# ODE stage of a convolution-attention hybrid: matmuls that stream 28 columns, 24 of them zeros, in place of 4

## The reference, cut to what matters

```python
def _mlp(y, W1, b1, W2, b2, W3, b3):
    h = jnp.tanh(y @ W1.T + b1)
    h = jnp.tanh(h @ W2.T + b2)
    return h @ W3.T + b3

def _rk4_step(y, dt, params):
    f = lambda z: _mlp(z, *params)
    k1 = f(y)
    k2 = f(y + dt / 2 * k1)
    k3 = f(y + dt / 2 * k2)
    k4 = f(y + dt * k3)
    return y + dt * (k1 + 2 * k2 + 2 * k3 + k4) / 6
```

## Time and profile before

| what | value |
|---|---|
| runs of the kernel, median (lowest to highest) | 7657.05 us (7656.08 to 7659.73) |
| the profiled execution, its own time | 7654.61 us |
| the profiled execution, span from first to last instruction | 7652.8 us |
| mean granted PE clock | 0.567 |
| busy: PE, DVE, ACT, POOL | 6975.1, 4228.9, 3810.8, 1229.8 us |
| matmuls at L851 with H, L851 with L, and L830 | 130816, 8176, 57232 |

### The profile page before, as it was taken

How to read it: one execution, slowest core, us unless ns; L and a number is a source line. 1 busy time by engine, 2 the same in 40 slices (tenths; PEclk the granted TensorE clock), 3 DMA queues, 4 the chain that set the end, 5 groups by cost and what they waited for, 6 DMA issues and landing times. The chain is left out here.

```text
span 7652.8 us, 407459 instructions
## 1 busy us (share of the span) xinstructions
PE 6975.1 (91%) x201629; PEld 6431.8 (84%) x144393; DVE 4228.9 (55%) x21034; ACT 3810.8 (50%) x26434; POOL 1229.8 (16%) x5230
## 2 busy tenths in 40 slices
PE   8884999999999999999999999999999998638886
PEld 3221999999999999999999999999999997427774
DVE  5444555555555555555555555555555554448997
ACT  3331555445544554455445554455445543328886
POOL 1000222112211221222112221122112221010001
PEclk7785555555555555555555555555555555658897
DMA  1000000100010001000100001000100000012332
GB/s 49 1 20 30 4 4 4 43 5 4 4 43 5 4 4 43 5 4 4 43 5 4 4 4 43 5 4 4 43 5 4 4 23 5 0 53 111 121 123 81
DMA packets 45001, 186.93 MB, mean 24 GB/s; under 512 B 7155, under 2 KB 27318, under 8 KB 33030
## 3 DMA queue, kind: packets, MB, share of 16 engines
q1 hardware_dynamic: 38662, 145.18, 4.9%
q0 software_dynamic: 4480, 15.38, 0.6%
HBM read 122.93 MB, written 37.62 MB: 21 GB/s over the span
## 5 line engine op out<-in xcount | busy, mean ns | idle before, releaser
L851 PE MATMUL p<-H,W 128*128 128x4 f16 x130816 | 5594.8, 168 | 36.7 <-ACT h L938 20.3
L851 PEld LDWEIGHTS p<-H,W 128*128 128x128 f16 x130816 | 5577.0, 105 | 51.0 <-ACT h L938 17.3
L830 PE MATMUL p<-L,W 128*128 128x4 f16 x57232 | 5157.8, 164 | 17.7 <-issue 17.7
L1012 DVE TENSOR_TENSOR_SCAN L<-H,h 128x8 f16<-128x8 f16 x12264 | 2210.6, 181 | 2615.3 <-ACT h L938 1561.9
L938 ACT ACTIVATE H<-p 128x4 f16<-128x4 f32 x6132 | 1093.9, 179 | 1416.3 <-PE p L830 1193.9
L945 ACT ACTIVATE H<-p 128x4 f16<-128x4 f32 x6132 | 1087.6, 178 | 1401.4 <-DVE p L1024 892.9
L851 PE MATMUL p<-L,W 128*128 128x4 f16 x8176 | 1369.3, 167 | 14.5 <-issue 12.0
L938 ACT ACTIVATE h<-p 128x4 f32<-128x4 f32 x6132 | 1046.0, 171 | 4.8
L945 ACT ACTIVATE h<-p 128x4 f32<-128x4 f32 x6132 | 1044.7, 171 | 0.0
L851 PEld LDWEIGHTS p<-L,W 128*128 128x128 f16 x8176 | 850.4, 104 | 37.4 <-issue 30.8
L804 POOL TENSOR_TENSOR twice<-r 128x16 f32<-128x16 f32 x511 | 109.2, 214 | 2425.9 <-DVE r L1021 2425.9
(11 more groups left out here) (379 smaller groups left out, 4609.3 us busy)
## 6 DMA issues: line engine op xcount, KB each, us to landing
e_W<-w_scaled SPq DMA_DIRECT2D x23, 2304.0 KB
e_W<-w_scaled SPq DMA_DIRECT2D x23, 1152.0 KB, 5.2
raw_f<-in_spline SPq DMA_DIRECT2D x21, 1024.0 KB, 6.8
w_scaled<-raw_f SPq DMA_DIRECT2D x7, 2304.0 KB, 9.0
w_scaled<-raw_f SPq DMA_DIRECT2D x7, 1152.0 KB, 11.2
raw<-in_spline POOLq DMA_DIRECT2D x3, 1024.0 KB, 7.1
rows_in<-zeros POOLq DMA_DIRECT2D x4, 768.0 KB, 12.0
e_xs<-rows_in SPq DMA_DIRECT2D x12, 256.0 KB, 5.8
```

The lines of the kernel that those rows point to most:

```text
L830: return pe.add_instruction(mybir.InstMatmult(name=nc.get_next_instruction_name(), engine=pe.engine, ins=[pe.lower_ap(x), pe.lower_ap(weig ...
L851: ins = pe.matmul(out[:, m, 0:B], weights, x[:, columns, 0], start=False, stop=(left[m] == 0 and part != "hl"), skip_group_check=True)
L1012: sg.up(dve.tensor_tensor_scan(flat(cols(L, GROUPS[n])), flat(cols(H, GROUPS[n])), flat(cols(h, GROUPS[n])), -1.0, ALU.mult, ALU.add), f"l ...
```

## The change

Each moving operand gets 28 columns. H1, H2, L1 and L2 become arrays of seven copies of their old shape; copy 0 is the one that ACT and DVE write and read as before, and copies 1 to 6 are set to zero once and never written again. A matmul takes the 4 columns of its chunk from all seven copies and writes columns 0 to 27 of the output chunk's bank, of which columns 4 to 27 begin at zero and get zeros added. The other readers of PSUM still take columns 0 to 3. The operand of the clearing matmuls is widened from 4 to 28 columns too. The memsets of the high slots' neighbours become memsets of the four whole arrays, and the counts that wait for `zeros` grow by two, or for PE to five. A local helper `wide` in the code of DVE is renamed `spread`.

```diff
+    PADS = 7
...
-        r, y1, b2s, zero = ..., sb("zero", [P, B], F16)
+        r, y1, b2s, zero = ..., sb("zero", [P, PADS * B], F16)
...
-        H1, H2 = sb("H1", [P, NV, 2], F16), sb("H2", [P, NV, 2], F16)
+        H1, H2 = sb("H1", [P, PADS, NV, 2], F16), sb("H2", [P, PADS, NV, 2], F16)
...
-        L1, L2 = sb("L1", [P, NV, 2], F16), sb("L2", [P, NV, 2], F16)
+        L1, L2 = sb("L1", [P, PADS, NV, 2], F16), sb("L2", [P, PADS, NV, 2], F16)
...
+        wide = lambda x: x[:, 0:PADS * B].rearrange("p (a b) -> p a b", b=B)
...
-            for x in (H1, H2):
-                sg.up(pool.memset(x[:, :, 1], 0.0), "zeros")
+            for x in (H1, H2, L1, L2):
+                sg.up(pool.memset(x[:], 0.0), "zeros")
...
-                ins = pe.matmul(out[:, m, 0:B], weights, x[:, columns, 0], start=False, ...)
+                ins = pe.matmul(wide(out[:, m]), weights, x[:, :, columns, 0], start=False, ...)
                 if part == "hl":
-                    ins = times_loaded(pe, out[:, m, 0:B], weights, L[:, columns, 0], left[m] == 0)
+                    ins = times_loaded(pe, wide(out[:, m]), weights, L[:, :, columns, 0], left[m] == 0)
...
-            sg.wait(pe, "zeros", 1)
+            sg.wait(pe, "zeros", 5)
...
-                    ins = pe.matmul(x[:, m, 0:B], W2[:, 0, m, 0:P], zero[:], start=True, stop=True)
+                    ins = pe.matmul(x[:, m, 0:PADS * B], W2[:, 0, m, 0:P], zero[:], start=True, stop=True)
...
-                                for x in (H1, h1):
+                                for x in (H1[:, 0], h1):
...
-                                for x in (H2[:, :, 0], h2[:, e, :, 0]):
+                                for x in (H2[:, 0, :, 0], h2[:, e, :, 0]):
...
-                sg.up(dve.tensor_tensor_scan(flat(cols(L, GROUPS[n])), flat(cols(H, GROUPS[n])), ...), f"lo{layer}")
+                sg.up(dve.tensor_tensor_scan(flat(cols(L[:, 0], GROUPS[n])), flat(cols(H[:, 0], GROUPS[n])), ...), f"lo{layer}")
```

More of the change, by code:

```diff
@@ L741, in flow @@
         wb3, hb = sb("wb3", [P, KH]), sb("hb", [P, NV])
-        r, y1, b2s, zero = sb("r", [P, 4, NV]), sb("y1", [P, NV]), sb("b2s", [P, NV]), sb("zero", [P, B], F16)
+        r, y1, b2s, zero = sb("r", [P, 4, NV]), sb("y1", [P, NV]), sb("b2s", [P, NV]), sb("zero", [P, PADS * B], F16)
         third, minus, twice, base = sb("third", [P, NV]), sb("minus", [P, NV]), sb("twice", [P, NV]), sb("base", [P, NV])
@@ L850, in product @@
                 x = L if part == "l" else H
-                ins = pe.matmul(out[:, m, 0:B], weights, x[:, columns, 0], start=False, stop=(left[m] == 0 and part != "hl"), skip_group_check=True)
+                ins = pe.matmul(wide(out[:, m]), weights, x[:, :, columns, 0], start=False, stop=(left[m] == 0 and part != "hl"), skip_group_check=True)
                 if part == "hl":
-                    ins = times_loaded(pe, out[:, m, 0:B], weights, L[:, columns, 0], left[m] == 0)
+                    ins = times_loaded(pe, wide(out[:, m]), weights, L[:, :, columns, 0], left[m] == 0)
                 if owed and all(left[c] == 0 for c in owed[0]):
@@ L926, in _ @@
                     sg.up(act.activation(split(q), full, ACT.Copy), "part")
-            sg.wait(act, "zeros", 3 + 1 + 4)
+            sg.wait(act, "zeros", 5 + 1 + 4)
             def steps(scale, factor):
@@ L964, in _ @@
             sg.wait(dve, "v_ps", 1)
-            wide = lambda x: x.rearrange("p (m o) -> p m o", o=1).to_broadcast([P, KH, B])
+            spread = lambda x: x.rearrange("p (m o) -> p m o", o=1).to_broadcast([P, KH, B])
             sg.seq(dve, dve.tensor_copy(wb3[:], pv[:, NV:NV + KH]), "prep")
@@ L970, in _ @@
             sg.seq(dve, dve.tensor_scalar(b3dt[:], b3[:], DT, None, ALU.mult), "prep")
-            sg.seq(dve, dve.tensor_tensor(mb(y1[:]), mb(pv[:, 0:NV]), wide(b1[:]), ALU.add), "prep")
+            sg.seq(dve, dve.tensor_tensor(mb(y1[:]), mb(pv[:, 0:NV]), spread(b1[:]), ALU.add), "prep")
             sg.seq(dve, dve.tensor_reduce(wmax[:, 0:1], w2f[:].rearrange("p k n -> p (k n)"), AX.X, ALU.max, apply_absolute_value=True), "scales")
@@ L991, in _ @@
                 sg.seq(dve, dve.tensor_scalar(coefs[:, n:n + 1], py[:, 1:2], C / WMAX * c, None, ALU.mult), "scales")
-            sg.seq(dve, dve.tensor_scalar(mb(hb[:]), wide(wb3[:]), wup[:, 1:2], None, ALU.mult), "prep")
-            sg.seq(dve, dve.tensor_scalar(mb(b2s[:]), wide(b2[:]), wup[:, 0:1], None, ALU.mult), "prep")
+            sg.seq(dve, dve.tensor_scalar(mb(hb[:]), spread(wb3[:]), wup[:, 1:2], None, ALU.mult), "prep")
+            sg.seq(dve, dve.tensor_scalar(mb(b2s[:]), spread(b2[:]), wup[:, 0:1], None, ALU.mult), "prep")
             sg.wait(dve, "probe_ps", 1)
@@ L1007, in _ @@
             dve.tensor_copy(sums(p2), mb(b2s[:])).then_inc(sg.sem["ready"], 1)
-            sg.wait(dve, "zeros", 3 + 1 + 4)
+            sg.wait(dve, "zeros", 5 + 1 + 4)
             def low(H, h, L, layer, e, n, w):
                 wait(dve, f"h{layer}", 2 * (G * e + n + 1), w)
-                sg.up(dve.tensor_tensor_scan(flat(cols(L, GROUPS[n])), flat(cols(H, GROUPS[n])), flat(cols(h, GROUPS[n])), -1.0, ALU.mult, ALU.add), f"lo{layer}")
+                sg.up(dve.tensor_tensor_scan(flat(cols(L[:, 0], GROUPS[n])), flat(cols(H[:, 0], GROUPS[n])), flat(cols(h, GROUPS[n])), -1.0, ALU.mult, ALU.add), f"lo{layer}")
             with dve.Fori(0, STEPS // UN) as i:
```

## The result

The changed kernel takes 7525.23 us (7524.01 to 7526.57, four runs) against 7656.57 us of the kernel before in the same comparison: ratio 0.9828, 95% interval 0.9811 to 0.9845. It is faster by 131 us, or 1.7%, in the forecast direction, but by just under half of the 265 us that were forecast. The time lies inside the stated range, and by only 10 us inside the forecast's own range, which ended at 7535 us.

The account below looks back on a forecast made before the run. A loop through PE, ACT and DVE (0.73 us plus 24 slots, 1.37 us a product) was taken as the bound; -66 ns x 4088 = -270, +5 at turns: 7392 us. Forecast's own range 7290 to 7535, stated range 7285 to 7745.

Parts of the forecast that it names:

- The clock: TensorE's granted clock in the ODE stage rises from 0.50 to 1.00, except some 10 us at each of seven turns.
- a clock that stays: Rival 1: in the ODE stage the granted clock does not leave 0.50, making the kernel slower; chance 0.15.
- The 24 slots: Matmul starts from the 24th to the product's last: spacing falls from 26.7 to 25 ns, -40 ns a product.
- rival 2: Slots follow the array clock: 13.3 ns each, saving 320 ns in 24 slots, between 6.3 and 6.9 ms; chance 0.08.
- The latency of the last matmul: From a product's last matmul to its result: -14 ns a product, bounds -37 to +8.
- the sign that the prediction had named: Time from last matmul to tanh of the last chunk: 0.20 us before, 0.19 forecast, 0.22 for rival 1.
- From load to matmul: Where PE resumes after its pause, a slot's worth of load shrinks from 26.7 to 13.3 ns: -12 ns, bounds 0 to -13.
- The sum: All terms of one product's loop together: -66 ns of 1367, narrowed range -90 to -31.
- Overlap of loads and streams: On PE, loads cover the longer streaming of 28 columns, so that slots do not grow.
- rival 3: Loads and streams on PE do not overlap: matmuls start near 50 ns apart; chance 0.04.
- Memsets, clearing matmuls and the scaling of expert weights: Work outside the loop or in DVE's idle time: memsets cost nothing, clearing under 0.2 us, scaling fits a 0.34 us gap.
- the mixed form: In the ODE stage the clock goes up and down by turns: -23 ns a product, 7563 us; chance 0.07.

Follow-up runs that it names:

- e8: Changed kernel with six copies, so 24 columns in each matmul instead of 28: 7707.39 us, ratio 1.0065 to the kernel before.
- e3: Changed kernel with twelve copies, so 48 columns in each matmul instead of 28: 7558.19 us, ratio 0.9876 to the kernel before.
- e4: Changed kernel with only the last of a product's 48 matmuls back at 4 columns: 7476.81 us, ratio 0.9768 to the kernel before.
- e1: Changed kernel with matmuls 1 to 47 back at 4 columns, only the last at 28: 7720.38 us, ratio 1.0091 to the kernel before.
- e6: Changed kernel with matmuls reordered (42 loads), the wait for L behind a pair's first matmul, and a 4-column last matmul: 7386.81 us, ratio 0.9648.
- e7: The order and moved wait of e6 without zeros, 4 columns in every matmul: 7417.86 us, ratio 0.9695 to the kernel before.
- e9: Changed kernel with a third matmul order (33 loads), the moved wait for L and a 4-column last matmul: 7155.96 us, ratio 0.9347.

## Why the prediction was half right

**The clock.** Right: 1.00 after the 761st microsecond but for 146 us in short stretches, with zeros as data; the prediction had put 70 us, at the turns. What these stretches cost is small either way: by its own terms 70 us come to 3.4 us, not 5, and 146 us at the measured difference of 33 ns in 1334 to 3.6. What the earlier trace rows show is a clock of 1.00 just behind matmuls of 512 columns without a gap; that 28 columns would do the same was the author's estimate, which no run of the kernel before shows. The clock was 1.00 with 28 columns and 0.50 with 24 (e8), so that 28 were enough was partly luck, and the chance of 0.15 for a clock that stays was not too high.

**The 24 slots.** Right in size. Six matmuls in a row take 0.30 us with 0.174 each, (0.30 - 0.174) / 5 = 25.2 ns, and the 579 ns of the table are 23 x 25.2; 24 x (26.7 - 25.2) = 36 ns, where 40 were forecast. (The prediction's (0.30 - 0.17) / 5 gives 26.0 as it is written; its 26.7 is right by the table, 614 / 23.) That the slots would stay at 26.7 is out, and so is rival 2. The 25 ns of the forecast were an estimate, as no f16 matmul of the kernel before runs at clock 1.00; the changed kernel shows 25.2 and e3 25.1.

**The latency of the last matmul: this is the step that failed.** The forecast was -14 ns: +8 for the columns and -22 because "the rest falls from 0.21 to 0.16" in f32 matmuls, of which half was taken over to f16. Measured is +10 by the recorded times, 164 to 174 ns, and +11 by the way from the last matmul to the tanh, 201 to 212 ns: the sign that the prediction had named, with 0.19 us for the forecast, shows 0.21. With 4 columns the recorded times are 164 and 165 ns at the two clocks, and the way to the tanh is 201 at both: the fixed part of these f16 matmuls does not shrink at all. The term thus lay a little above its upper bound of +8. No run shows that +8 itself, an estimate of the author for 28 columns against 4, nor the 3 taken off the 168: what the runs show at clock 1.00 is 201 ns to the tanh with 4 columns (e4), 212 with 28 (changed kernel) and 219 with 48 (e3), and at 0.50 it is 201 with 4 (the kernel before) and 217 with 28 (e1). The f32 rows of 512 columns were the wrong neighbour; why they lose 45 ns and these lose nothing stays open.

**From load to matmul.** Forecast -12. From the 24th to the 25th matmul it is 39 ns where it was 48; 1.5 of the 9 are the shorter slot, so that some -8 are left for this term, inside its bounds.

**The sum.** -36 + 11 - 8 = -33 ns, as the medians have it (1334 against 1367), with -32 from the counts of matmuls, and against -66 forecast. Of the 33 ns that are missing the latency has 25, the slots 4 and the load 4. The prediction had narrowed the forecast's range to -31 at the weak end on the ground that no two terms would be at their ends, and the measured sum is just there; that it stayed inside is luck, as one term was beyond its end. The count of matmuls in 200 us, 7380 by the forecast, is 7185.

**The rest.** Overlap of loads and streams: right, a slot did not grow (25.2 ns, 34 loads in 48 slots), so rival 3 is out; its figure near 50 was an estimate that no run shows. Memsets, clearing matmuls and the scaling of expert weights cost nothing that shows: the steady loop, 4088 x 33 = 135 us, accounts for all 131. For a clock that stays and for the mixed form the author had estimated 20 ns a product for the 24 columns, +82 us, which no run shows; e1 gives +67 (57 to 83), with the tanh 16 ns later.

## What to carry to other kernels

The higher granted clock helped only a part of the loop here: 1.5 ns of each slot and some 8 ns at one pause, while the 201 ns from a 4-column matmul to its tanh, ACT, DVE and the signals kept their times; draw the loop of dependences first and change only its clocked part. Padding that fell short of raising the clock was pure loss here (+30 and +49 us), so look at the granted clock of the stage in every variant, and keep the matmul whose result is waited for narrow (46 us here). Where a loop passes through a wait, moving that wait by one instruction can be worth as much as the higher clock: 7523.54 us without zeros, against 7525.23 with them.

## What the runs showed of the hardware that was not expected

- The recorded time of an f16 matmul of 4 columns is 164 ns at clock 0.50 (e1) and 165 at 1.00 (e4), and from its start to the start of the tanh that waits for it the median is 201 ns at both (the kernel before, e4).
- Matmuls of 28 and of 48 columns both start 25 ns apart at clock 1.00 (changed kernel, e3); at 0.50 matmuls of 4 and of 24 columns keep the same pace, 26.7 ns (23 slots in 614 ns in the kernel before, in 613 in e8).
- With 28 columns, 24 of them zeros, the granted clock of 1800 to 2000 us was 1.00; with 24 columns, 20 of them zeros, it was 0.50 (e8).
- With 90 loads and matmuls in about 1.30 us PE pauses for 0.2 to 0.6 us again and again at either clock, more often at the higher one (e6, e7), and it does not with 81 in 1.24 us (e9). What it waits for stays open.
